# First attention: q and k as two float32r parts, two heads to a stack, matmuls issued in pairs

## The reference

```python
qkv = einsum('oc,bct->bot', qkv_w, normed) + qkv_b        # normed: layer norm, then group norm
q, k, v = split(qkv, 3, axis=1)                           # 8 heads of ch = 16 channels
q = (q * scale).reshape(b * 8, 16, t); k = (k * scale).reshape(b * 8, 16, t)
weight = softmax(einsum('bct,bcs->bts', q, k), axis=-1)   # 1024 x 1024 for each of 64 heads
a = einsum('bts,bcs->bct', weight, v)
out = einsum('oc,bct->bot', proj_w, x + a) + proj_b
```

## Time and profile before

| | us |
|---|---|
| median of 3 executions | 2272.27 (2271.85 to 2276.23) |
| the profiled execution | 2275.42 |
| its span, first to last instruction | 2273.5 |
| stage one ends, attention stage starts | 168.3 |
| first score matmul of image 0 | 221.3 |
| last score matmul of image 7 | 1054.5 |

### The profile page before, as it was taken

The page is one execution under the profiler, slowest core; times in us unless marked ns, Lnnn a source line. Parts: engine busy times, 40 slices in busy tenths (PEclk is TensorE's granted clock), DMA queues, the critical chain, the costliest instruction groups (busy, mean ns, idle before and its releaser), DMA issues. The chain is left out here.

```text
span 2273.5 us, 41046 instructions
## 1 busy us (share of the span) xinstructions
PE 1929.1 (85%) x13306; PEld 1073.3 (47%) x13307; DVE 1436.2 (63%) x3154; ACT 1098.7 (48%) x1682; POOL 755.4 (33%) x883
## 2 busy tenths in 40 slices
PE   5769999999999999998589996996659992699993
PEld 2331223332332323232367774554447661599992
DVE  4769888888888888871346665762235665344444
ACT  4550665666666666666144442541225551344442
POOL 0232003343333333345335553000001667355551
PEclk9875999999999999999699998999879996799995
DMA  3851532323232323012333333322100242233326
GB/s 127 193 217 33 78 55 29 60 35 65 31 66 29 66 29 66 2 38 63 105 86 99 95 99 119 111 84 61 38 29 29 62 136 81 71 94 92 90 72 229
DMA packets 134782, 180.00 MB, mean 79 GB/s; under 512 B 44592, under 2 KB 87856, under 8 KB 132336
## 3 DMA queue, kind: packets, MB, share of 16 engines
q1 hardware_dynamic: 116208, 138.25, 25.6%
q0 software_dynamic: 18432, 39.88, 5.2%
HBM read 99.04 MB, written 69.01 MB: 74 GB/s over the span
## 5 line engine op out<-in xcount | busy, mean ns | idle before, releaser
L779 DVE TENSOR_REDUCE mx<-bank 128x1 f32<-128x512 f32 x1024 | 639.7, 696 | 86.4 <-PE bank L550 85.2
L726 ACT ACTIVATE P<-bank 128x1024 f32<-128x1024 f32 x512 | 497.4, 1021 | 313.1 <-PE bank L652 312.9
L550 PE MATMUL bank<-ks,qs 96*128 96x512 bf16 x1024 | 358.6, 402 | 35.5 <-DVE mx L779 35.5
L1290 POOL DMA_INDIRECT results<-yo,places x284 | 274.1, 965 | 283.6 <-DVE yo L1280 236.8
L652 PE MATMUL bank<-qs,ks 99*128 99x512 bf16 x1024 | 308.2, 384 | 2.6 <-ACT P L726 1.8
L1206 PE MATMUL bank<-xt,up 128*128 128x256 f32 x1136 | 274.8, 386 | 3.7 <-DVE xt L1257 1.4
L632 PE MATMUL bank<-P,vt 128*32 128x512 f32 x2048 | 272.8, 605 | 0.7 <-ACT P L726 0.7
L2289 POOL DMA_INDIRECT dispatched<-planes,places x128 | 124.5, 973 | 420.2 <-DVE stats L2133 357.3
L1206 PEld LDWEIGHTS bank<-xt,up 128*128 128x128 f32 x1136 | 207.5, 193 | 30.4 <-issue 4.7
L550 PEld LDWEIGHTS bank<-ks,qs 96*128 96x128 bf16 x1024 | 99.8, 98 | 257.5 <-DVE mx L779 177.7
L652 PEld LDWEIGHTS bank<-qs,ks 99*128 99x128 bf16 x1024 | 78.0, 97 | 280.0 <-ACT P L726 182.8
(11 more groups left out here) (298 smaller groups left out, 2581.8 us busy)
## 6 DMA issues: line engine op xcount, KB each, us to landing
xr<-dispatched SPq DMA_DIRECT2D x142, 130.0 KB
qk_parts<-parts SPq DMA_DIRECT2D x16, 768.0 KB, 5.1
qs<-qk_parts SPq DMA_DIRECT2D x84, 128.0 KB
ks<-qk_parts SPq DMA_DIRECT2D x84, 128.0 KB
v_turned<-vt SPq DMA_DIRECT2D x8, 1024.0 KB, 5.6
vt<-v_turned SPq DMA_DIRECT2D x8, 1024.0 KB
bands<-results SPq DMA_DIRECT2D x32, 256.0 KB, 3.7
y<-results SPq DMA_DIRECT2D x32, 256.0 KB
```

The lines of the kernel that those rows point to most:

```text
L550: pe.matmul(bank[:, slot, :], qs[par][0:KB, h, c * C:(c + 1) * C], ks[par][0:KB, h, half * HALF:(half + 1) * HALF], start=True, stop=True) ...
L726: act.activation(P[:, x % SLOTS, :], bank[:, 2 * pair:2 * pair + 2, :] .rearrange("p a t -> p (a t)"), ACT.Exp).then_inc(probs_ready, 1)
L779: dve.tensor_reduce(mx[:, k // 2, k % 2:k % 2 + 1], bank[:, slot, :], AX.X, ALU.max).then_inc(unit_freed, 1)
L1290: pool.indirect_dma_start(yd_dram, bass.IndirectOffsetOnAxis(places[:, p, q:q + 1], 0), yo[:, p, q, :], None).then_inc(sent[p], 16)
```

## The change

q and k are split in two parts of 12 bits of mantissa, held in f32 words as float32r: ACT writes the rounded value, one subtraction writes the remainder. The stack of a head is 3 x 16 = 48 rows (high-high, high-low, low-high), and 2 rows for the maximum. Two heads share a stack column: one on rows 0 to 49, one on rows 64 to 113. The stacks become `[128, 4 pairs, 1024]` in f32. Score matmuls of two heads, and now also maxima of two heads, stand next to each other on the two halves of the rows. A pair of maxima waits once, for both its banks. `STEP_OF` deals pairs instead of single maxima, so a step has two to six maxima. The third-part operations of stage one and of `split_rows` are gone. The memsets of ones are 32 rows of each half, for the first stack in stage one and for the second at the start of the attention stage.

```diff
-Q_PARTS = (0, 0, 0, 1, 1, 2)
-K_PARTS = (0, 1, 2, 0, 1, 0)
+Q_PARTS = (0, 0, 1)
+K_PARTS = (0, 1, 0)
 KB = len(Q_PARTS) * CH
-KM = KB + 3
+KM = KB + 2
+PAIRS = HEADS // 2
+ROWS = C // 2
...
+    eng.tensor_copy(parts[:, 0].bitcast(F32R), value).then_inc(done, 1)
+    eng.wait_ge(done, b * 2 + 1)
+    eng.tensor_tensor(parts[:, 1].bitcast(F32R), value, parts[:, 0], ALU.subtract).then_inc(done, 1)
+
+
+def stack_rows(u, r):
+    return slice(u * ROWS + r * CH, u * ROWS + (r + 1) * CH)
...
+            sp.wait_ge(ones_set, 2)
             for r, (qp, kp) in enumerate(zip(Q_PARTS, K_PARTS)):
                 for s, part, stack in ((0, qp, stacks0[0]), (1, kp, stacks0[1])):
+                    for u in range(2):
+                        sp.dma_start(stack[stack_rows(u, r)],
+                                     parts_dram[0, s, part].rearrange("(p u i) t -> u i p t", u=2, i=CH)[u]).then_inc(stacks_loaded, 16)
...
-                if db is not None:
-                    for s, rest_ready in enumerate((q_rest, k_rest)):
-                        act.wait_ge(rest_ready, db + 1)
-                        act.activation(parts[:, 1 - p, s, 1], rest[:, s], ACT.Copy).then_inc(second_parts, 1)
...
-                        act.activation(parts[:, p, s, 0], qk[:, s], ACT.Copy).then_inc(first_parts, 1)
+                        act.activation(parts[:, p, s, 0].bitcast(F32R), qk[:, s], ACT.Copy).then_inc(first_parts, 1)
...
+        def split(eng, s, b, p, ready):
+
             eng.wait_ge(first_parts, b * 2 + s + 1)
+            eng.tensor_tensor(parts[:, p, s, 1].bitcast(F32R), qk[:, s], parts[:, p, s, 0], ALU.subtract).then_inc(ready, 1)
...
-                if db is not None:
-                    split_last(dve, 0, db, 1 - p, q_split)
...
         def _(pool):
+            for u in range(2):
+                pool.memset(stacks0[1][u * ROWS + 32:(u + 1) * ROWS], 1.0).then_inc(ones_set, 1)
+                pool.wait_ge(ones_set, u + 1)
...
-STEP_OF = {unit: index * STEPS // len(BODY_UNITS) for index, unit in enumerate(BODY_UNITS)}
+BODY_GROUPS = [unit for unit in BODY_UNITS if unit[0] != "max" or unit[1] % 2 == 0]
+STEP_OF = {unit: index * STEPS // len(BODY_GROUPS) for index, unit in enumerate(BODY_GROUPS)}
+STEP_OF.update({("max", k): STEP_OF["max", k - 1] for k in range(1, MAXIMA, 2)})
...
-                for part in range(3):
...
+                for u in range(2):
+                    for part in range(2):
+                        row = u * ROWS + KB + part
...
-                pe.matmul(bank[:, slot, :], qs[par][0:KB, h, c * C:(c + 1) * C],
-                          ks[par][0:KB, h, half * HALF:(half + 1) * HALF], start=True, stop=True).then_inc(unit_filled, 1)
+                pe.matmul(bank[:, slot, :], qs[par][rows, pair, c * C:(c + 1) * C].bitcast(F32R),
+                          ks[par][rows, pair, half * HALF:(half + 1) * HALF].bitcast(F32R), start=True, stop=True).then_inc(unit_filled, 1)
...
-                            head = 4 * g + 2 * pair + u
-                            ins = pe.matmul(bank[:, 2 * pair + u, :], ks[par][:, head, s * C:(s + 1) * C],
-                                            qs[par][:, head, n * HALF:(n + 1) * HALF], start=True, stop=True)
+                            rows_of = slice(u * ROWS, u * ROWS + KM)
+                            ins = pe.matmul(bank[:, 2 * pair + u, :], ks[par][rows_of, 2 * g + pair, s * C:(s + 1) * C].bitcast(F32R),
+                                            qs[par][rows_of, 2 * g + pair, n * HALF:(n + 1) * HALF].bitcast(F32R), start=True, stop=True)
                         ins.then_inc(scores_ready, 1)
-                        for index, (kind, k) in now[:2] if pair == 0 else now[2:]:
+                        for index, (kind, k) in now[:first_half(now)] if pair == 0 else now[first_half(now):]:
                             slot = 5 + index % 3
-                            pe.wait_ge(unit_freed, base + max(index - 2, 0))
+                            if kind != "max":
+                                pe.wait_ge(unit_freed, base + max(index - 2, 0))
+                            elif k % 2 == 0:
+                                pe.wait_ge(unit_freed, base + max(index - 1, 0))
```

More of the change, by code:

```diff
@@ L8 @@
 BF16 = mybir.dt.bfloat16
+F32R = mybir.dt.float32r
 ALU = mybir.AluOpType
@@ L339, with maximum, first_half @@
 BODY_UNITS = units_of_a_body()
-STEP_OF = {unit: index * STEPS // len(BODY_UNITS) for index, unit in enumerate(BODY_UNITS)}
+BODY_GROUPS = [unit for unit in BODY_UNITS if unit[0] != "max" or unit[1] % 2 == 0]
+STEP_OF = {unit: index * STEPS // len(BODY_GROUPS) for index, unit in enumerate(BODY_GROUPS)}
+STEP_OF.update({("max", k): STEP_OF["max", k - 1] for k in range(1, MAXIMA, 2)})
+def maximum(k):
+    pair, c, half, u = k // 32, k // 4 % TC, k // 2 % 2, k % 2
+    return pair, c, half, u
+def first_half(now):
+    return 2 if now and now[0][1][0] == "max" else 1
 def of_next(unit):
@@ L463, in max_rows @@
             def max_rows(b, par, g):
-                sp.wait_ge(rows_split, b * 8 + 4 * g + 4)
-                for part in range(3):
-                    sp.dma_start(qs[par][KB + part:KB + part + 1, 4 * g:4 * g + 4, :]
-                                 .rearrange("p h (c t) -> p (h c) t", t=C),
-                                 nm_parts[:, part, :]).then_inc(rows_loaded, 16)
+                sp.wait_ge(rows_split, b * 4 + 2 * g + 2)
+                for u in range(2):
+                    for part in range(2):
+                        row = u * ROWS + KB + part
+                        sp.dma_start(qs[par][row:row + 1, 2 * g:2 * g + 2, :].rearrange("p h (c t) -> p (h c) t", t=C),
+                                     nm_parts[16 * u:16 * u + 16, part, :]).then_inc(rows_loaded, 16)
             def blank_rows_at(sp, n):
@@ L545, in take_max @@
             def take_max(b, par, k, slot):
[L547 removed]
+                pair, c, half, u = maximum(k)
+                rows = slice(u * ROWS, u * ROWS + KB)
                 if k % 64 == 0:
                     pe.wait_ge(qk_loaded[k // 64], b * LOADS)
[L550 to L551 removed]
+                pe.matmul(bank[:, slot, :], qs[par][rows, pair, c * C:(c + 1) * C].bitcast(F32R),
+                          ks[par][rows, pair, half * HALF:(half + 1) * HALF].bitcast(F32R), start=True, stop=True).then_inc(unit_filled, 1)
             def project(b, n, slot):
@@ L778, in reduce @@
                 dve.wait_ge(unit_filled, filled)
-                dve.tensor_reduce(mx[:, k // 2, k % 2:k % 2 + 1], bank[:, slot, :], AX.X, ALU.max).then_inc(unit_freed, 1)
+                pair, c, half, u = maximum(k)
+                row = 32 * (pair // 2) + 16 * u + 8 * (pair % 2) + c
+                dve.tensor_reduce(mx[:, row, half:half + 1], bank[:, slot, :], AX.X, ALU.max).then_inc(unit_freed, 1)
                 if k % 64 == 63:
@@ L1052, in first @@
             def first():
-                for par in range(2):
-                    pool.memset(ks[par][KB:KM, :, :], 1.0).then_inc(ones_set, 1)
-                pool.wait_ge(ones_set, 2)
+                for u in range(2):
+                    pool.memset(ks[1][u * ROWS + 32:(u + 1) * ROWS], 1.0).then_inc(ones_set, 1)
+                    pool.wait_ge(ones_set, u + 1)
                 split_rows(0, 0, FIRST_UNITS.index(("rows", 0)) + 1)
```

78 lines of the change are left out of this document (29 added, 49 removed).

## The result

The changed kernel takes 2371.55 us (median of 4, 2361.93 to 2384.99) against 2272.06 beside it: a ratio of 1.044, 95% interval 1.038 to 1.050. It is slower, and near the 2382 of the forecast. The profiled execution is the fastest of the four, 2361.93 with a span of 2360.0 at a mean granted clock of 0.874; the others had 0.863 to 0.873, and the lower the clock the longer the time. The ratios of the experiments leave out executions that lie well above the fastest of their kernel, which matters in e1 alone: there two of four go, and 1.028 would be 1.039 by the median of all.

A forecast was written before the change was run, and what follows sets the result against it. A loop of PE and DVE waits, 2.93 us a step, bounds attention. 2275.4 - 20 (stage one) + 12 (first maxima) + 3 (full-clock attention) + 115 (clock) = 2385, 2382 on the median's scale; range 2205 to 2500.

The forecast's parts named there:

- A pair in the new form: Score or maximum pair on PE: float32r at bf16 pace, two on separate rows overlap; a pair costs 0.22 instead of 0.43.
- B: float32r matmuls stream at the f32 transposes' pace, pairs overlapping: +0.61 us a step, 2437 us in all; chance 0.15.
- C: float32r matmuls run as full f32, two records each: +490 us and more, about 2790 us; chance 0.06.
- D: Matmuls on separate rows do not overlap: step 3.35 us, +108 us, about 2370 us; chance 0.04.
- The weights: f32 weight load on PE exposed behind the weighing matmuls and before the second maxima pair: 0.10 us in each place.
- The loop: PE and DVE waiting for each other in an attention step: 2.91 us instead of 2.93, -5 us over 256 steps.
- Uneven steps and shapes: Attention steps of two to six maxima and PE array-shape switches: 1 us an image, +8 us in eight images.
- First maxima: 80 maxima before image 0: a pair every 1.50 us against 1.20 for two reductions, +12 us over 40 pairs.
- Stage one: Third-part operations removed, shorter waits and a smaller memset before attention: -20 us in sum, ends -8 and -30.
- both DVE terms: In stage one, a removed DVE subtraction, -8.5 us over 7 images, and `normed` perhaps missing a POOL subtraction, -4 us.
- The clock: PE's granted clock falls to half in attention's routing steps and most of image 0: +115 us, between 0 and 228.
- Rival A: Attention keeps full clock: 2267 us with exposed weight loads, 2212 us with hidden ones; chance 0.25.

The follow-up runs named there:

- e1: Changed kernel, with the first matmul of every pair of maxima but a step's first issued twice more, on its 48 rows: 2359.35 us, ratio 1.0279.
- e4: Changed kernel, with both maxima of a pair on the same half of the rows, so they cannot overlap: 2604.59 us, ratio 1.1471.
- e9: Changed kernel, with the first maxima of a step issued ahead of both score pairs: 2290.74 us, ratio 1.0087.
- e11: Kernel before (bf16), with the first maxima of a step issued ahead of both score pairs: 2243.66 us, ratio 0.9873.
- e7: Changed kernel, with four maxima in each step instead of two to six: 2316.59 us, ratio 1.020.
- e6: Kernel before, with its maxima made on 32 rows of the 96, same number, columns and order of matmuls: 2439.73 us, ratio 1.0743.
- e2: Kernel before (bf16), with only the changed kernel's deal of units to steps and one wait per pair of maxima: 2340.03 us, ratio 1.0307.
- e5: Changed kernel, with one unused f32 matmul on all 128 rows before every pair of maxima but a step's first: 2329.22 us, ratio 1.0247.
- e3: Changed kernel, with each maximum waiting for its own bank again: 2383.22 us, ratio 1.0512.
- e10: Changed kernel, with four maxima in each step, a wait per maximum, and first maxima ahead of both score pairs: 2229.93 us, ratio 0.981.

## Why the prediction was right

The outline of the forecast is what happened: a step that stays as long as it was, a clock that no longer holds, stage one's gain and the loss in the first maxima. The reason that it gave for the clock did not hold, two terms were mis-sized in opposite directions, and that the total came as near as 10 us is in part luck. Step by step:

- **A pair in the new form.** Right. A float32r matmul of 512 columns is 0.39, the bf16 one's 0.38, and two on separate rows start together. Rivals B, C and D fall with it, and e4 gives the overlap's worth by itself.
- **The weights.** Right: the load is exposed behind W and behind the wait, 0.50 against 0.40, which is the 0.10 taken. The load's own record is 0.19 for 0.10.
- **The loop.** 2.94 measured, 2.91 forecast, 2.93 before. e9 and e11 show that the loop is real: taking S out of it gave 0.23 and 0.10.
- **Uneven steps and shapes**, forecast +1 an image. This term was mis-sized: "the number of reductions in the loop is the same in sum" holds, but a step with two maxima too many costs 1.27 (4.21 for 2.94) and one with two too few gives back less: 0.5 in each of the projection steps, which PE's other work bounds (9.5 for e7's 10.6). 3.7 an image, and e7 shows it to be the deal.
- **First maxima.** Pairs every 1.57 where 1.50 was forecast; 40 x 0.37 = 15, less 3.4 for the shorter memset (7.07 for two on POOL, DVE's copy 3.46: as forecast) is the +12 seen, where 12 - 3.4 = 9 was forecast.
- **Stage one.** -20 as forecast, but not by its parts. The last projection of q and k started at 145.2 and now at 127.2, -18 where -12.5 was forecast for both DVE terms; the end of the stage gave 2 instead of 4, and the memset's 3.4 belongs to the next stage.
- **The clock.** Half-clock steps are 4.59 (forecast 4.42). The clock fell in the routing steps of images 1 to 6, as forecast, but also at the start of an image and around step 11, and it did not wait for the projection: no stretch at half ended in one, the longest of images 1 to 6 lasted 20.5 us, and those of the routing steps were over by step 23, where 20 steps an image were taken. Image 0, taken at half in all of its steps, was so for 22 of 107 us. 227 us at half are about 50 steps' worth; they cost some 75 us (64, and most of images 0 and 7), where +115 was taken. That +115 was the middle between nothing and 228 and no sum of its own. The two errors cancel in part: the order +19 too low, the clock 40 too high. The profiled execution came out 23 below its 2385, and the median lies 10 above that execution.
- **Rival A** is the outcome by the rule of the Trainium skill, TensorE: Matmul & The Clock Gate (Part 1), which ties the fall to the array being idle; the trace does not agree. In e6 and e4 it stayed at half with PE busy 64.50 of 64.50 and 104.37 of 106.00 us. The same evidence corrects the reason that the forecast gave, that PE streams 1.72 of 2.91: e2 keeps the clock and e6 loses it with the same columns in a step of the same length, and filling PE's gap with 48-row matmuls helped in one execution of four (e1), with 128-row ones in all (e5).

What stays open: which quantity the clock follows exactly (rows, rows by columns, or the values that are multiplied, which change with the rows); the runs only order the kernels, and e6 also changes heights from matmul to matmul. And e3's lower clock than the changed kernel's, with the same matmuls, has no explanation here.

## What to carry to other kernels

When two engines wait for each other in a ring of banks, draw the loop before making an operation faster: here halving both products gave nothing, and moving two lines, so that independent work lies in the wait, gave 0.10 to 0.24 us a step. A matmul that uses fewer rows, or two that overlap, does the same products with less of the array at work, and the granted clock can take back what the shape gave; read the clock of the stage before and after. Here it took back all that the shape gave in attention, so compare a new form with the old one in the same order (e10 with e11), stage by stage, before calling it a gain. Deal work so that no step has more of it than its neighbours on the engine that is nearly the bound.

## What the runs showed of the hardware

- float32r of 512 columns has the pace of bf16: 0.39 us a record, 0.23 from one to the next where the rows are the same (e4's pairs, 0.73 against 0.50), and an f32 weight load of 0.19 against 0.10 for bf16.
- A PE without idle time in its records can stay at half clock: 64.50 busy of 64.50 us in e6, 104.37 of 106.00 in e4.
- A matmul on 32 rows after one on 99, or the other way, loses 0.10 us (e6); 96 after 99 and 48 after 50 lose nothing.
- Four executions of one kernel differed by 2.2% in time with clocks of .875 to .904 (e1), and by 3.1% with .764 to .798 (e4), where the kernel before stays within 0.6%. A low clock does not do it alone: e6, at .860, spread by 0.3%, and e5, at .906 to .911, by 0.4%.
